# Exact first edges for groups of 32 nodes, and nine tiles of edges a group, in a graph layer on one core

## The reference

```python
h = maximum(layernorm(x), 0)
m = h[src] + edge_attr                               # 206250 x 96
aggr = segment_sum(m, dst, num_segments=6250)
hidden = relu(aggr @ W1 + b1)                        # 192 wide
out = x + (1.0 + eps) * h + hidden @ W2 + b2
```

## Time and profile before

| what | value |
|---|---|
| median of 3 runs | 544.64 us (542.91 to 547.36) |
| the profiled execution, whole | 548.56 us |
| its span, first to last instruction | 546.7 us |
| granted TensorE clock, mean | 0.977 |
| PE busy | 484.3 us, 89% |
| DVE busy | 485.0 us, 89% |
| ACT busy | 419.3 us, 77% |
| POOL busy | 338.7 us, 62% |
| moved by DMA | 120.56 MB, 221 GB/s over the span |

### The profile page before, as it was taken

How to read it: one execution, slowest core, us unless ns; L and a number is a source line. 1 busy time by engine, 2 the same in 40 slices (tenths; PEclk the granted TensorE clock), 3 DMA queues, 4 the chain that set the end, 5 groups by cost and what they waited for, 6 DMA issues and landing times.

```text
span 546.7 us, 23317 instructions
## 1 busy us (share of the span) xinstructions
PE 484.3 (89%) x9560; PEld 461.0 (84%) x9560; DVE 485.0 (89%) x712; ACT 419.3 (77%) x637; POOL 338.7 (62%) x200
## 2 busy tenths in 40 slices
PE   0426899999999959999999899999999999999995
PEld 0315889999999949998999799999889999999994
DVE  7996999999999868889999779799999989999960
ACT  0798687888887828887988578879786888888771
POOL 1310002888888877886888558878887888880000
PEclk9997899999999989999999899999999999999998
DMA  6789988988888987999899569999976888987000
GB/s 185 255 279 252 258 278 269 287 246 210 238 246 218 251 225 204 281 252 268 222 252 231 157 177 264 250 286 247 263 208 173 220 224 240 225 216 230 6 10 19
DMA packets 99110, 120.56 MB, mean 221 GB/s; under 512 B 71161, under 2 KB 72793, under 8 KB 98871
## 3 DMA queue, kind: packets, MB, share of 16 engines
q1 hardware_dynamic: 74854, 108.13, 64.5%
q0 software_dynamic: 24144, 10.89, 15.7%
HBM read 112.50 MB, written 6.48 MB: 218 GB/s over the span
## 4 chain that ended last, share of the span: by engine, by line
PE 54%; POOL 16%; SPq 13%; issue 8%; DMA 3%; DVE 3%; ACT 2%; ACTq 0%; DVEq 0%; POOLq 0%
PE agg_ps L1027 20%; PE oct_ps L1015 14%; POOL gathered_edges L496 14%; PE agg_ps L1021 11%; SPq L355 4%; PE key_ps L1039 4%; SPq L356 3%; PE mlp_ps L1044 3%; SPq L354 3%; POOL win L464 2%; ACT adj L864 1%; DMA gathered_edges<-h_rows,gather_src 1%; DMA gathered_edges<-in_dst 1%; SPq L363 1%; SPq L364 1%
## 5 line engine op out<-in xcount | busy, mean ns | idle before, releaser
L864 ACT ACTIVATE adj<-oct_ps 128x784 f16<-128x784 f32 x360 | 299.6, 865 | 87.7 <-PE oct_ps L1015 83.0
L496 POOL DMA_INDIRECT gathered_edges<-h_rows,gather_src x160 | 300.3, 1877 | 66.4 <-issue 45.4
L1027 PE MATMUL agg_ps<-hl,adj 128*128 128x192 f16 x2205 | 234.7, 247 | 1.7 <-issue 1.5
L567 DVE TENSOR_TENSOR lo_hot<-iota_z,key 128x2048 f16<-128x2048 f16 x180 | 219.6, 1220 | 0.0
L1015 PE MATMUL oct_ps<-z,lo_hot 128*128 128x98 f16 x2880 | 192.5, 210 | 14.4 <-DVE lo_hot L567 6.6
L567 DVE TENSOR_TENSOR z<-z_marks,key 128x1568 f16<-128x1568 f16 x180 | 174.6, 970 | 9.3 <-PE oct_ps L1015 9.3
L1015 PEld LDWEIGHTS oct_ps<-z,lo_hot 128*128 128x128 f16 x2880 | 166.3, 100 | 17.5 <-issue 7.6
L1027 PEld LDWEIGHTS agg_ps<-hl,adj 128*128 128x128 f16 x2205 | 174.6, 98 | 4.0 <-issue 1.6
L1021 PE MATMUL agg_ps<-edges,hot 128*32 128x96 f32 x3600 | 87.6, 251 | 8.0 <-issue 5.6
L1021 PEld LDWEIGHTS agg_ps<-edges,hot 128*32 128x32 f32 x3600 | 76.9, 112 | 13.3 <-issue 6.1
L464 POOL DMA_INDIRECT win<-packed_keys,row_i x23 | 32.8, 1425 | 72.5 <-DMA gathered_edges<-in_edge_attr 61.3
(11 more groups left out here) (126 smaller groups left out, 185.0 us busy)
## 6 DMA issues: line engine op xcount, KB each, us to landing
edges<-in_edge_attr SPq DMA_DIRECT2D x180, 480.0 KB
gathered_edges<-in_edge_attr SPq DMA_DIRECT2D x16, 480.0 KB
dst<-in_dst SPq DMA_DIRECT2D x180, 5.0 KB
gathered_edges<-h_rows,gather_src POOLq DMA_INDIRECT x160
out<-ob SPq DMA_DIRECT2D x45, 48.0 KB
packed_keys<-adj SPq DMA_DIRECT2D x1, 1632.0 KB, 6.7
h_rows<-gathered_edges SPq DMA_DIRECT2D x1, 1200.0 KB, 10.0
h_rows<-gathered_edges SPq DMA_DIRECT2D x1, 1152.0 KB, 9.0
```

The source lines that it names most:

```text
L496: nc.gpsimd.indirect_dma_start(out=gathered[k][:, g, t, :], out_offset=None, in_=h_dram, in_offset=bass.IndirectOffsetOnAxis(ap=gather_src ...
L567: return nc.vector.tensor_tensor(out.rearrange("p t (w two) -> p t w two", two=2), marks[0:out.shape[0], 0:width].rearrange("p (o w two) - ...
L864: return nc.scalar.activation(adj[k][:, :, 2 * OCT * o:2 * OCT * (o + 1)].rearrange("p h (t q) -> p t h q", q=2), oct_ps[:, o % 2, :].rear ...
L1027: last = nc.tensor.matmul(agg_ps[buf][:, 0:2 * C], adj[buf][:, h, :], hl[:, h, :], start=False, stop=(h == NT - 1), skip_group_check=True)
```

## The change

`GT` goes from 10 to 9: a group's load holds 1152 edges. The largest group of these inputs has 1148. Loading from up to 32 edges ahead would miss some, so the table becomes exact. The row of each group's last sample is worked out for 200 groups in two halves of 100 (`SPLIT`) by two small products on PE; POOL fetches for each group the 32 destinations of that row by an indirect DMA; DVE counts those below the group's first node, adds the count to 32 times the row, and PE turns the column into a row for `e_tab`. SP waits for the first half before block 0 and for both before block 3. The old table stays for the general loop. `passes_needed` gets six operations more. The residual is done in seven pieces (13 rows, then six of 6), since `h` now lies 36 tiles deep in the first gathered buffer; this moves the load of gathered block 1 from behind block 14 to behind block 12. POOL's windows come every 23/3 gathers instead of 25/3, and it issues 144 gathers in all instead of 160.

```diff
-GT = 10
+GT = 9
+SPLIT = 100
-FETCH_EVERY = 25
+FETCH_EVERY = 23
-RES_FIRST = 40
-RES_ROWS = 5
+RES_FIRST = 36
+RES_ROWS = 6
...
+            sp.wait_ge(tab_ready, SPLITS)
             for b in range(TURN, NM):
...
-            pool.wait_ge(row_ready, 1)
-            pool.wait_ge(keys_stored, 16)
-            for q in range(WINS):
-                fetch(q)
+            pool.wait_ge(group_rows_ready, 1)
+            for q in range(max(WINS, SPLITS)):
+                if q < SPLITS:
+                    nc.gpsimd.indirect_dma_start(out=group_ids[:, q, :], out_offset=None, in_=dst[0:FULL * STEP].rearrange("(r e) -> r e", e=STEP),
+                                                 in_offset=bass.IndirectOffsetOnAxis(ap=group_row_i[:, q:q + 1], axis=0)).then_inc(group_ids_in[q], 16)
+                if q == 0:
+                    pool.wait_ge(row_ready, 1)
+                    pool.wait_ge(keys_stored, 16)
+                if q < WINS:
+                    fetch(q)
...
+            v.wait_ge(group_rows_done, 1)
+            nc.vector.tensor_scalar(group_row_i[:, :], agg_ps[0][0:SPLIT, 0:SPLITS], float(FULL - 1), None, ALU.min).then_inc(group_rows_ready, 1)
+            nc.vector.tensor_scalar(group_row[:, :], agg_ps[0][0:SPLIT, 0:SPLITS], float(FULL - 1), None, ALU.min)
...
-            chain(nc.vector.tensor_scalar(e_raw[:, :], oct_ps[:, 0, 0:GCOLS], float(STEP), None, ALU.mult))
-            nc.vector.tensor_scalar(e_tab[:, :], e_raw[:, :], float(ELAST), None, ALU.min).then_inc(tab_ready, 1)
...
+            def exact_starts(k):
+                v.wait_ge(group_ids_in[k], 16)
+                chain(nc.vector.tensor_tensor(group_less[:, k, :], group_ids[:, k, :], group_node[:, k:k + 1].broadcast_to([SPLIT, STEP]), ALU.is_lt))
+                chain(nc.vector.tensor_reduce(group_count[:, k:k + 1], group_less[:, k, :], AX_X, ALU.add))
+                nc.vector.scalar_tensor_tensor(group_start[:, k:k + 1], group_row[:, k:k + 1], float(STEP), group_count[:, k:k + 1],
+                                               ALU.mult, ALU.add).then_inc(group_start_ready, 1)
...
+            def start_table(k):
+                part = slice(SPLIT * k, SPLIT * (k + 1))
+                v.wait_ge(starts_turned, k + 1)
+                nc.vector.tensor_scalar(e_tab[:, part], agg_ps[1][0:1, part], float(ELAST), None, ALU.min).then_inc(tab_ready, 1)
+                nc.vector.tensor_copy(e_exact[:, part], agg_ps[1][0:1, part]).then_inc(spread_read, 1)
...
+            exact_starts(0)
             pick(0)
+            start_table(0)
             normal(1)
+            exact_starts(1)
+            nc.vector.tensor_scalar(e_raw[:, :], oct_ps[:, 0, 0:GCOLS], float(STEP), None, ALU.mult)
...
+            start_table(1)
...
+            def turn_starts(k):
+                pe.wait_ge(group_start_ready, k + 1)
+                nc.tensor.transpose(agg_ps[1][0:1, SPLIT * k:SPLIT * (k + 1)], group_start[:, k:k + 1], ident[0:SPLIT, 0:SPLIT]).then_inc(starts_turned, 1)
```

More of the change, by code:

```diff
@@ L63, in build @@
     GCOLS = PAIRS * 2 * GROUPS
+    SPLITS = GCOLS // SPLIT
+    FULL = E // STEP
+    assert SPLITS * SPLIT == GCOLS and SPLIT <= P
     SLOT_CUTS = [sum(SLOTS_AFTER[:o]) for o in range(OCTS + 1)]
@@ L153, in build @@
         e_raw = sb("e_raw", [P, GCOLS])
-        e_tab = sb("e_tab", [P, GCOLS], I32)
+        e_tab = sb("e_tab", [1, GCOLS], I32)
+        e_exact = sb("e_exact", [1, GCOLS])
+        exact_gap = sb("exact_gap", [1, GCOLS])
+        group_row = sb("group_row", [SPLIT, SPLITS])
+        group_row_i = sb("group_row_i", [SPLIT, SPLITS], I32)
+        group_node_i = sb("group_node_i", [SPLIT, SPLITS], I32)
+        group_node = sb("group_node", [SPLIT, SPLITS])
+        group_ids = sb("group_ids", [SPLIT, SPLITS, STEP], I32)
+        group_less = sb("group_less", [SPLIT, SPLITS, STEP])
+        group_count = sb("group_count", [SPLIT, SPLITS])
+        group_start = sb("group_start", [SPLIT, SPLITS])
         span = sb("span", [1, GCOLS])
@@ L228, in build @@
         tab_ready = sem("tab_ready")
+        group_rows_done = sem("group_rows_done")
+        group_rows_ready = sem("group_rows_ready")
+        group_ids_in = [sem(f"group_ids_in{k}") for k in range(SPLITS)]
+        group_start_ready = sem("group_start_ready")
+        starts_turned = sem("starts_turned")
         need_ready = sem("need_ready")
@@ L456, in _ @@
             nc.gpsimd.memset(ones[:, :], 1.0).then_inc(iotas, 1)
-            pool.wait_ge(iotas, 7)
+            nc.gpsimd.iota(group_node_i[:, :], [[SPLIT * GROUP, SPLITS]], base=0, channel_multiplier=GROUP).then_inc(iotas, 1)
+            pool.wait_ge(iotas, 8)
+            nc.gpsimd.tensor_copy(group_node[:, :], group_node_i[:, :])
             nc.gpsimd.tensor_copy(gbase[:, :], gbase_i[:, :])
@@ L552, in _ @@
             nc.vector.memset(x_sb[:, NT - 1, :], 0.0).then_inc(x_clear, 1)
-            v.wait_ge(iotas, 7)
+            v.wait_ge(iotas, 8)
             nc.vector.memset(hid[C:C + 1, 0, :], 1.0)
@@ L656, in passes_needed @@
             def passes_needed():
-                v.wait_ge(spread_read, 2)
+                v.wait_ge(spread_read, 2 + SPLITS)
                 nc.vector.tensor_scalar(row[:, :], row[:, :], keep[:, 0:1], None, ALU.mult)
@@ L671, in passes_needed @@
                 chain(nc.vector.tensor_scalar(need[:, 0:2], need[:, 0:2], 1.0, 1.0, ALU.add, ALU.max))
+                chain(nc.vector.tensor_scalar(exact_gap[:, :], e_exact[:, :], float(FULL * STEP), float(E - FULL * STEP), ALU.is_ge, ALU.mult))
+                chain(nc.vector.tensor_tensor(e_exact[:, :], e_exact[:, :], exact_gap[:, :], ALU.add))
+                chain(nc.vector.tensor_tensor(exact_gap[:, 0:NT * GROUPS], e_exact[:, 1:NT * GROUPS + 1], e_exact[:, 0:NT * GROUPS], ALU.subtract))
+                chain(nc.vector.tensor_reduce(need[:, 2:3], exact_gap[:, 0:NT * GROUPS], AX_X, ALU.max))
+                chain(nc.vector.tensor_scalar(need[:, 2:3], need[:, 2:3], float(GE), None, ALU.is_gt))
+                chain(nc.vector.tensor_tensor(need[:, 1:2], need[:, 1:2], need[:, 2:3], ALU.mult))
                 chain(nc.vector.tensor_tensor(need[:, 0:1], need[:, 0:1], need[:, 3:4], ALU.max))
@@ L1003, in _ @@
             pe.wait_ge(picked_ready, 1)
+            for k in range(SPLITS):
+                last = nc.tensor.matmul(agg_ps[0][0:SPLIT, k:k + 1], picked[:, 0, :, :].rearrange("p q k -> p (q k)")[:, SPLIT * k:SPLIT * (k + 1)], ones[:, 0:1],
+                                        start=True, stop=True)
+            last.then_inc(group_rows_done, 1)
+            pe.wait_ge(picked_ready, 3)
             for a in range(2):
@@ L1051, in next_keys @@
                 turn_keys(q % 2, q % WINS).then_inc(turned, 1)
+            def turn_starts(k):
+                pe.wait_ge(group_start_ready, k + 1)
+                nc.tensor.transpose(agg_ps[1][0:1, SPLIT * k:SPLIT * (k + 1)], group_start[:, k:k + 1], ident[0:SPLIT, 0:SPLIT]).then_inc(starts_turned, 1)
+            turn_starts(0)
             pe.wait_ge(spread_read, 1)
             next_keys(0)
+            pe.wait_ge(tab_ready, 1)
+            pe.wait_ge(spread_read, 2)
+            turn_starts(1)
             pe.wait_ge(w_in, 16 * 5)
@@ L1078, in next_project @@
                 project(hid, OUT_AT).then_inc(out_done, 1)
-            pe.wait_ge(spread_read, 2)
+            pe.wait_ge(spread_read, 2 + SPLITS)
             for b in range(NM):
```

2 lines of the change are left out of this document (1 added, 1 removed).

## The result

The changed kernel took 526.85 us in the median of its four runs (524.74 to 527.93), the kernel before 545.06 us beside them: a ratio of 0.967, 95% interval 0.963 to 0.971. Repeated on another chip with six runs it gave 0.969 (0.965 to 0.973). The gain is 17 to 18 us where 12.3 were forecast. The profiled execution took 525.82 us, 22.7 less than that of before (548.56), which lay 3.5 us above its own median; so a difference between the two traces overstates the gain by 4 to 5 us.

What follows compares the result with a forecast made beforehand. Blocks 2 to 10 were taken as DVE-bound at 10.26 us, later ones PE-bound at 10.00, beside holes. Terms 1.5 - 0.3 - 6.3 - 6.2 - 1.0 = -12.3 us gave 532.3 us; own range 528 to 535, wider range 526 to 539.

Steps and rivals of the forecast that it cites:

- The start: Ahead of block 0: exact table adds 2.6 us on DVE, 1.1 hidden, so 1.5 us more reach ACT.
- 1.5 us later than 34.85: Sign at the start: ACT's third square root begins 1.5 us later than the 34.85 of before.
- DVE-bound blocks: Blocks 2 to 10: seven residual pieces instead of nine and narrower one-hots take 0.3 us off.
- PE, -6.3: From block 11 on: 38 sums, each 0.167 us shorter by 8 fewer records, take 6.3 us off.
- Block 14: Hole of 8.2 us at block 14: gather no longer waited for, id wait of 2.0 at block 12; 6.2 us off.
- Lighter DMA: Later holes of about 13 us: rows of 3456 B instead of 3840 B gain 1.0 us.
- a chance of timing: Rival: the stretch at 310 us was chance that lighter DMAs remove; up to 5 us more, 527 us; chance 0.12.
- DMA share: Sign in a settled block: the DMA engines' share falls below 0.92; a rise would show the prediction wrong.
- The end: Six more linked operations, 1.8 us, ahead of a join waiting 2.59 us for PE: cost nothing.
- Slower, DMA bound by unaligned rows: Rival: unaligned rows take longer and DMA becomes the bound; at 20% dearer rows 571 us; chance 0.06.
- Pauses and late ids grow elsewhere: Rival: PE's pauses and late ids grow elsewhere, about 8 us back, 540 to 544 us, within 1%; chance 0.12.

Runs made afterwards that it cites:

- ten loaded, nine summed: Kernel before with the exact table, ten tiles loaded and gathered, but PE sums only nine of each group's ten tiles: 538.31 us, ratio 0.984.
- the experiment: Exact table, ten tiles loaded but nine gathered and summed (144 gathers): 531.95 us, 0.972 of the kernel before; with 160 gathers and nine summed 538.31 us.
- the rounded table: Kernel before with nine tiles, its old rounded table kept, so some edges are left out: 525.55 us, ratio 0.961 to the kernel before.
- the exact table with ten tiles: Changed kernel with ten tiles, 160 gathers and nine residual pieces again, only the exact table kept: 544.94 us, ratio 1.000 to the kernel before.
- setting the sums apart: Kernel before, with the own edge sum one octet later in the four blocks that also sum a gathered block: 543.05 us, ratio 1.000.

## Why the prediction came out as it did

The direction was right. The time lay inside the range of 526 to 539, though only by 0.9 us, 5.4 us below the forecast and outside the forecast's own 528 to 535. The gain was 18 us by the medians, where 12.3 were summed. Two steps promised too little (the start by 1.5 us, the holes by some 7), one too much (PE's rate by 1.7), so part of the nearness is luck. The steps in turn:

- **The start, +1.5: mis-sized, it cost 0.** DVE's wait for the two products was 0.20 us, not 0.5. While the ids were on their way DVE did layer-norm work, so no wait for them is seen; the key window was there too:

```profile
22.18 0.83 PE L1058 MATMUL agg_ps<-ones,hot 128*100 128x1 f32 x4 [2.86 <-DVE hot L656]
...
23.54 1.22 POOL L500 DMA_INDIRECT group_ids<-in_dst,group_row_i  x1 [3.59 <-DVE group_row_i L662]
...
23.05 0.16 DVE L662 TENSOR_SCALAR group_row_i<-agg_ps 100x2 int32<-100x2 f32 x1 [0.20 <-PE agg_ps L1058]
...
27.06 0.18 DVE L680 TENSOR_TENSOR group_less<-group_ids,group_node 100x32 f32<-100x32 int32 x1
27.28 0.18 DVE L681 TENSOR_REDUCE group_count<-group_less 100x1 f32<-100x32 f32 x1
...
28.07 0.25 DVE L688 TENSOR_SCALAR e_tab<-agg_ps 1x100 int32<-1x100 f32 x1
...
34.19 0.17 DVE L614 TENSOR_SCALAR stat<-stat 128x17 f32<-128x17 f32 x1
...
34.39 0.22 ACT L937 ACTIVATE rstd<-stat 128x17 f32<-128x17 f32 x1
```

  The ids were issued at 23.54 and used at 27.06. In the prediction DVE's extra work was 2.6 us, of which 1.1 were hidden. Here DVE hands over its last statistics at 34.36 (34.19 + 0.17), 0.6 us after the 33.75 of before, and ACT takes them at once, at 34.39, where it took them at 34.85 before. The whole start runs 0.5 us earlier in this trace (ACT's first scaling at 22.52 against 23.00), so DVE's extra is 1.1 us, just what lay hidden. What the sum had wrong is what comes off: DVE takes up the first count at 27.06, where `pick(0)` stood at 28.45, 0.9 us earlier with the 0.5 taken off, since two operations on the table and a wait of 0.41 us for PE ahead of them are gone; 2.0 us come back behind it. The sign "1.5 us later than 34.85" did not come.
- **DVE-bound blocks, -0.3: about right as to size.** Block 2 to 11 took 92.60 us against 92.45. The pieces of the residual are 6 of 809 ns and one of 1509, as forecast (815 and 1.52).
- **PE, -6.3: right in kind, 1.7 us too large.** From the gathered to the own sum of a block it is 1.51 us, where 1.67 was the earlier trace rows: 0.16 for 8 records, as taken. But a settled block fell by 0.12, not 0.167. At 0.12 over 38 sums the term is 4.6. DVE's one-hots are not what holds it: ten loaded, nine summed has the wide ones and is 9.89. The last 0.04 us of a block stays open.
- **Block 14, -6.2: right.** With the faster blocks the forecast for block 11 to 15 was 7.0 us off (6.2 and 5 x 0.167); 7.6 came. PE doesn't wait for the gather, and DVE waits 2.26 us for ids at block 12, 2.0 taken. The 16 gathers alone bring 6.4 us with ten tiles loaded, the experiment shows. POOL was early for one more reason than forecast: the 36th gather was issued at

```profile
175.24 2.02 POOL L524 DMA_INDIRECT gathered_edges<-h_rows,gather_src  x1 [0.90 <-PE agg_ps L1079]
```

  and not at 183.66 and the start's 1.5: before, three of POOL's issues up to there had lasted 4.0 to 4.5 us (one of them below), where this trace has none over 2.4. It is partly luck: the second profile of the changed kernel has one of 5.1 us, and its 36th gather was issued at 178.52, still in time.

```profile
157.42 3.97 POOL L464 DMA_INDIRECT win<-packed_keys,row_i  x1 [0.30 <-issue]
```

- **Lighter DMA, -1.0: the step that failed, by cause and by size.** From block 15 to 42 the traces differ by 16.6 us. Of these 27 x 0.12 and 3 x 0.16 are PE's rate, 3.7; so the holes lost are 12.9 us between the profiles, and some 8 by the medians, whose whole gain is 5 us less, if the difference lies there. Of the 12.9, 5.9 are PE's pauses of over 0.6 us with "issue" (four before, none after) and some 3 the clock behind the largest; the rest wasn't taken apart. The prediction read the pause at 310 us in PE's own row and then put its removal down to DMA weight, and, as a rival at 0.12, to "a chance of timing" that they remove; that rival's 527 us is the time that came, by another mechanism: fewer products on PE took the pause away with the bytes unchanged, and fewer bytes without that did not. What PE lacked in the pause were its own instructions, by the packets of q8.
- **DMA share.** Below 0.92, as said: 0.87 in the stretch and 0.90 over the settled blocks (0.92 in the second profile, against 0.95 before). The DMA time of a byte rose, though. On the loads' queue (q1 of the pages), share times span by MB is 3.24 to 3.29 us with ten tiles loaded (six profiles) and 3.36 to 3.42 with nine (eight profiles, the rounded table's too): some 4% more. So it comes with the rows of 3456 B and not with the exact starts: such rows, 13.5 times 256 B, begin off a multiple of 256 B every other time under either table, rows of 3840 B (15 times) don't. The Trainium skill ("DMA: Bandwidth & Descriptors", section "How a descriptor splits into AXI transactions") has a descriptor that starts between such multiples pay from the one below. As an estimate by it, 112 beats in place of 108 in every other row are 2%, of the edges alone; the trace agrees in sign and shows more than that, and no run here tried what the rest is. With ten tiles and the exact table it would ask 124 beats for 120 in every load from an odd edge (the 112 to 128 in that run's expectation are wrong for it); 0.94 for 248 GB/s shows none of that. The time followed neither.
- **The end, 0:** the six extra operations (starts 506.41 to 508.02) stand ahead of a join at 509.71 that still waits 0.64 us for PE; the cover held with 0.64 to spare of 2.59. The +1.1 us behind block 42 is as long as a pause of PE of the same kind as above, which ends 1.25 us after the landing of a packet of q8; before, none lies behind block 42's sum:

```profile
483.05 0.57 PE L1097 MATMUL key_ps<-aggT,w_sb 96*96 96x128 f32 x3 [1.11 <-issue]
```

- **The rivals.** "Slower, DMA bound by unaligned rows" is refuted by the time itself, and by the exact table with ten tiles (1.000). "Pauses and late ids grow elsewhere" didn't come: they shrank.

## What to carry over

A hole in the engine that sets the pace, with "issue" as its only releaser, belongs to that engine's own program: look for the landing of an instruction packet ahead of its end. It is to be priced by that engine's instruction count and not by the transfers of data; and it is worth more than its length, since the granted clock can fall with it. A hole in one profile is worth what the medians say: setting the sums apart took 4.6 us out of one block and nothing out of the time, and a gain of 2 to 4 us read from one chip's runs was gone on the next. When two kernels are compared for one cause, see that nothing else moved: the place of the twelve DMAs, not the bytes, was what set 15.17 us apart from 12.34. Where a chain of POOL gathers has to be ready for one block, count back from its last issue: 16 gathers fewer, 4 of them ahead of that block, brought 6.4 us, and 10% fewer bytes of edges nothing that is clear.

## What was not expected of the hardware

- PE paused 1.8 to 2.9 us in the middle of runs of matmuls with all operands there; seen in each of the five profiles with ten sums, in four of them inside the sum at block 24, in one (2.23) in another place. 33 of 36 such pauses of over 0.75 us, in all profiles, end 1.1 to 1.6 us after a 16 KB packet of the instruction queue q8 landed.
- With the pause of 2.70 us the granted clock fell to 0.50 and was 0.79 over the block, and with one of 2.87 us in another kernel it stayed at 1.00. What decides between them wasn't tried.
- Loads from any edge took no more of the DMA engines than loads from multiples of 32 edges; rows of 3456 B took some 4% more for a byte than rows of 3840 B.
- A gather on POOL lasts 1.84 to 1.88 us in the mean (144 and 160 of them), but single issues of POOL 4 to 5 us: three in each profile of the kernel before, two of them fetches of a key window (3.97 us), none and one in those of the changed kernel. Their cause wasn't looked for.
